# Sum of the expert outputs, normalisation and second projection in one block, the list in the experts' block, and semaphores cleared a stage later

## The reference

```
scores = softmax(x @ router_w + expert_bias); top_w, top_idx = top_k(scores, 4); top_w /= sum(top_w)
out_k  = (silu(x @ gate[k]) * (x @ up[k])) @ down[k]            # 16 experts
ffn    = sum over the 4 chosen k of top_w[k] * out_k
x      = x + layernorm(ffn)                                      # layer 2
h      = layernorm(x); q, k, v = h @ Wq.T, h @ Wk.T, h @ Wv.T    # 32 heads of 8
f      = log_sigmoid(h @ Wf.T + bf); c = cumsum(f)               # float32
scores = q k / sqrt(8) + c_i - c_j, causal, softmax, times v, @ Wo.T
```

## Time and profile before

| | |
|---|---|
| runs | 1692.95, 1695.21, 1696.98 us; median 1695.21 |
| profiled execution | 1693.19 us, of which the span is 1691.2 us |
| mean granted TensorE clock | 0.788 of full |
| busy over the span | PE 1168.4, DVE 1196.8, ACT 886.3, POOL 422.6 us |
| router | 513.2 to 564 us |
| expert loop | 567 to 768 us |
| combine, n2, clear, qkv1 | 774.4 to 923.2 us |
| attention a1 | 923.2 to 1450 us |

### The profile page before, as it was taken

How to read it: one execution, slowest core, us unless ns; L and a number is a source line. 1 busy time by engine, 2 the same in 40 slices (tenths; PEclk the granted TensorE clock), 3 DMA queues, 4 the chain that set the end, 5 groups by cost and what they waited for, 6 DMA issues and landing times. The chain is left out here.

```text
span 1691.2 us, 26266 instructions
## 1 busy us (share of the span) xinstructions
PE 1168.4 (69%) x7624; PEld 567.9 (34%) x7701; DVE 1196.8 (71%) x3589; ACT 886.3 (52%) x1731; POOL 422.6 (25%) x565
## 2 busy tenths in 40 slices
PE   2456555556532599991183899999999999737995
PEld 1112221122221366660151233333333333323664
DVE  4799999999848444445647888888888887355443
ACT  2698898888761243332341366566666666233212
POOL 0212212221114577771120122222222222010000
PEclk9655555555555799995587799999999999768997
DMA  2255665666514122226065111111111110201001
GB/s 66 82 120 115 125 132 110 117 129 119 98 44 93 41 78 79 78 80 217 0 241 196 54 38 58 57 39 57 57 40 56 58 41 29 78 0 23 1 1 50
DMA packets 221546, 130.96 MB, mean 77 GB/s; under 512 B 167990, under 2 KB 194742, under 8 KB 221150
## 3 DMA queue, kind: packets, MB, share of 16 engines
q1 hardware_dynamic: 200942, 100.17, 23.8%
q0 software_dynamic: 6320, 15.54, 2.9%
q10 hardware_dynamic: 14144, 13.57, 2.8%
HBM read 54.51 MB, written 40.76 MB: 56 GB/s over the span
## 5 line engine op out<-in xcount | busy, mean ns | idle before, releaser
L884 ACT ACTIVATE a_probs<-a_st 128x1024 f32<-128x1024 f32 (+3 forms) x256 | 212.4, 865 | 158.5 <-PE a_st L816 158.5
L938 DVE CUSTOM_DVE_ANT_0 a_unread<-a_row,all_mask 128x128 bf16<-128x128 f32 (+3 forms) x512 | 238.7, 485 | 32.8 <-PE a_row L781 28.0
L781 PE MATMUL a_row<-l_k,a_q 128*128 128x512 bf16 (+3 forms) x736 | 229.9, 334 | 45.4 <-DMA l_k<-k_rows 27.3
L816 PE MATMUL a_st<-a_q,l_k 128*128 128x384 bf16 (+3 forms) x735 | 224.0, 327 | 26.4 <-ACT a_probs L884 24.3
L653 DVE CUSTOM_DVE_ANT_0 a_rows<-a_sc,all_mask 128x128 bf16<-128x128 f32 (+7 forms) x256 | 191.5, 748 | 22.1 <-PE a_sc L507 21.1
L912 POOL TENSOR_SCALAR_AFFINE_SELECT a_probs<-a_probs 128x256 f32<-128x256 f32 x256 | 102.5, 406 | 412.3 <-ACT a_probs L884 336.3
L556 ACT ACTIVATE a_rows<-a_rows 128x128 bf16<-128x128 bf16 (+7 forms) x256 | 173.2, 677 | 61.1 <-DVE a_rows L663 57.1
L942 DVE TENSOR_REDUCE a_mx<-a_row 128x1 f32<-128x512 f32 x256 | 175.9, 687 | 38.4 <-PE a_row L781 38.4
L507 PE MATMUL a_sc<-a_k,a_q 16*128 16x512 bf16 (+3 forms) x384 | 167.2, 504 | 49.8 <-DVE a_mx L653 43.1
L835 PE MATMUL a_o<-a_probs,a_v 128*32 128x384 f32 (+3 forms) x1920 | 176.6, 431 | 0.0
L565 ACT ACTIVATE a_unread<-a_rows 128x128 bf16<-128x128 bf16 (+7 forms) x256 | 170.7, 667 | 0.0
(11 more groups left out here) (247 smaller groups left out, 1849.2 us busy)
## 6 DMA issues: line engine op xcount, KB each, us to landing
a_q<-q_rows SPq DMA_DIRECT2D x64, 128.0 KB
l_k<-k_rows SPq DMA_DIRECT2D x64, 128.0 KB
o_rows<-a_oT SPq DMA_DIRECT2D x32, 256.0 KB, 2.0
a_turned_sb<-a_rows SPq DMA_TRANSPOSE x256, 2.6
sum_made<-out_rows SPq DMA_DIRECT2D x8, 512.0 KB, 9.3
sum_made<-out_rows ACTq DMA_DIRECT2D x8, 512.0 KB, 8.5
a_raw<-in_gate ACTq DMA_DIRECT2D x16, 224.0 KB, 3.4
a_raw<-in_up ACTq DMA_DIRECT2D x16, 224.0 KB, 4.1
```

Source lines behind the costliest of these rows:

```text
L781: nc.tensor.matmul(row[:, n % SLOTS, 0:w], q_sb[:, u % RING, POS[qb] * P:(POS[qb] + 1) * P], k_sb[:, u % RING, h, lo:lo + w], start=True, ...
L816: last = nc.tensor.matmul(st[:, n % 2, to + first:to + end], k_sb[:, u % RING, h, kb * P:(kb + 1) * P], q_sb[:, u % RING, first:end], star ...
L884: nc.scalar.activation(probs[:, n % GR, lo:hi], st[:, n % 2, lo:hi], ACT.Exp).then_inc(exp_done, 1)
L938: nc.vector.tensor_tensor_reduce(out=unread[:, n % SLOTS, 0:w], in0=tile[:, 0:w], in1=mask[:, at:at + w], scale=1.0, scalar=-3e38, op0=ALU ...
```

## The change

1. Instead of `clear`, `retire()` only sets the semaphores of the stages so far aside. `wipe(pool)`, a call within POOL's queue of a later stage, clears them: after the first memset of the experts' block, after the memsets of the new sum block, after the first copy of attention a1, and at the end of POOL's queue in the int8 network. The clear at the very end stays.
2. `router` and `experts` are one Block. PE waits on `which_ready` before the loop. The four operations that make `chosen` are the function `weigh()`, called in DVE's loop ahead of tile 4. Part of SBUF and PSUM is shared between list and loop.
3. The eight constant stores of the tails are in the experts' block, on SP between the tables and the down weights, with a wait for their landing ahead of the down weights.
4. `combine`, n2 and `qkv1` become `sum_and_project`. Tiles are taken in the order in which the attention wants its blocks (`tile_at`), in four groups of four; statistics, root and normalisation are per group (`Spread`), the second normalisation is on ACT. The orders of the queues are written out by hand. Items of q and k go by batch half. The gate is on 64 partitions x 1024. ACT now rounds straight from PSUM to the first part, DVE subtracts it from PSUM: two DVE operations and two ACT operations per item, where there were four and one. Stores go per 512 columns; q is stored in three planes only. All loads are issued by SP, the weights after four tiles.
5. `load` of attention a1 reads planes 0 and 1 of q more than once: eight transfers per unit instead of four.

```diff
-        clear(nc)                       # three places
+        retire()
...
+def wipe(pool):
+    for s in Core.stale:
+        pool.sem_clear(s)
...
@@ experts
+            tails(sp)
             sp.dma_start(wd[:], ...).then_inc(wd_loaded, 16)
...
+            pe.wait_ge(which_ready, 1)
+            for i in range(TILES + 3):
...
             nc.gpsimd.memset(every[:], 1.0).then_inc(ones_set, 1)
+            wipe(pool)
...
+            nc.vector.tensor_scalar(which[:], endsum[:], float(E - 1), None, ALU.min).then_inc(which_ready, 1)
             for i in range(TILES + 1):
+                if i == 4:
+                    weigh()
...
@@ sum_and_project, SP
+            for p in range(GT): load(p)
+            (weights)
+            for p in range(GT, T): load(p)
+            for i in range(len(todo)):
+                store(i)
+                if i == len(todo) - 5:
+                    sp.wait_ge(f_chain, 7)
+                    sp.dma_start(c_v[:, 0:3], cparts[:]).then_inc(c_stored, 16)
@@ PE, per half s
+                turn(2 * s); gate(2 * s)
+                if s + 1 == B: turn(2 * s + 1); gate(2 * s + 1)
+                project(first); project(first + 1); value(2 * s)
+                if s + 1 < B:
+                    turn(1); gate(1); project(2); project(3); value(1); project(4 .. 7)
+                else:
+                    project(10 .. 15); value(3)
@@ PE, project(i)
+                if i >= 2: pe.wait_ge(remains, i - 1)
@@ ACT
+            def norm_y(g):
+                act.wait_ge(of_y.nmi_ready, g + 1)
+            def round_high(i):
+                act.wait_ge(acc_ready, i + 1)
+                nc.scalar.mul(parts[:, i % pring, 0], acc[:, i % 2], scale[todo[i][0]]).then_inc(high, 1)
+            def round_middle(i):
+                act.wait_ge(remains, i + 1)
+                nc.scalar.copy(parts[:, i % pring, 1], rest[:, i % pring]).then_inc(middle, 1)
+            def split_pair(i): round_high(i); round_high(i + 1); round_middle(i); round_middle(i + 1)
+            scale_first(0), scale_first(1), norm_y(0), scale_first(2), norm_y(1), norm_x(0), copy_x(0),
+            scale_first(3), split_pair(0), copy_v(0), norm_x(1), norm_y(2), copy_x(1), split_pair(2),
+            copy_v(1), norm_x(2), norm_y(3), split_pair(4), split_pair(6), copy_x(2), norm_x(3), copy_x(3),
+            split_pair(8), copy_v(2), gate_step(0 .. 3), split_pair(10), (12), (14), copy_v(3)
@@ POOL
+            wipe(pool)
+            of_y.root(0), of_y.root(1), of_x.root(0), of_y.root(2), of_x.root(1), of_y.root(3), of_x.root(2), of_x.root(3)
@@ DVE
+            def less_high(i):
+                dve.wait_ge(high, i + 1)
+                nc.vector.scalar_tensor_tensor(out=rest[:, i % pring], in0=acc[:, i % 2], scalar=scale[todo[i][0]],
+                                               in1=parts[:, i % pring, 0], op0=ALU.mult, op1=ALU.subtract).then_inc(remains, 1)
+            def less_middle(i):
+                dve.wait_ge(middle, i + 1)
+                nc.vector.tensor_tensor(out=parts[:, i % pring, 2], in0=rest[:, i % pring], in1=parts[:, i % pring, 1],
+                                        op=ALU.subtract).then_inc(low, 1)
+            def split_pair(i): less_high(i); less_high(i + 1); less_middle(i); less_middle(i + 1)
+            combine(0), invert y0, combine(1), residual(0), invert y1, x0, combine(2), residual(1), invert y2, x1,
+            split_pair(0), combine(3), residual(2), invert y3, x2, split_pair(2), residual(3), invert x3,
+            split_pair(4), (6), (8), gate_step(0 .. 6), split_pair(10), (12), (14)
...
@@ attention a1, load
-                for sb, rows in ((q, q_rows), (k[:, h], k_rows)):
-                    sp.dma_start(sb[64 * h:64 * (h + 1), :], rows (8 planes x 8 rows))
+                for first, count, plane in ((0, 3, 0), (3, 2, 1)):
+                    sp.dma_start(q[64 * h + first * hd:64 * h + (first + count) * hd, :],
+                                 q_v[plane:plane + 1].broadcast_to([count, hd, S])).then_inc(sem, 16)
+                sp.dma_start(q[64 * h + 5 * hd:64 * (h + 1), :], q_v[5:8]).then_inc(sem, 16)
+                sp.dma_start(k[64 * h:64 * (h + 1), h, :], k_v).then_inc(sem, 16)
```

More of the change, by code:

```diff
@@ L1305, in gather_of, with experts @@
     return gather
-def router(nc, a, lg, wd, wd_loaded, chosen, which, source, target, gather):
+def experts(nc, a, lg, wparts, wd, wd_loaded, chosen, which, source, target, taken, gathered, gather, ident_f, ident_b, out_rows, tails):
     with ExitStack() as ctx:
-        c = Core(nc, ctx, "route")
+        c = Core(nc, ctx, "moe")
         later = c.sb("later", [P, P], BF16)
@@ new lines, with tile_at, natural_pieces, projections @@
+STORES = {"q": 2, "k": 3}
+def tile_at(p):
+    return p // TB * TB + ORDER[p % TB]
+def natural_pieces(j):
+    out = []
+    for m, blk in enumerate(range(4 * j, 4 * j + 4)):
+        if out and POS[blk] == out[-1][2] + out[-1][1]:
+            out[-1][1] += 1
+        else:
+            out.append([m, 1, POS[blk]])
+    return out
+def projections():
+    out = []
+    for s in range(B):
+        out += [("q", s, j, ch) for j in range(2) for ch in range(KC)]
+        out += [("k", s, j, ch) for j in range(2) for ch in range(KC)]
+    return out
@@ L1658, in _ @@
         @block.scalar
         def _(act):
-            for t in range(1, ring, 2):
-                load(act, t)
-            for t in range(T):
-                act.wait_ge(loaded[t % ring], 16 * (t // ring + 1))
-                if t >= 2:
-                    act.wait_ge(added, 3 * (t - 1) - 2)
-                nc.scalar.activation(part[:, t % 2, 0], made[:, t % ring, 0, :], ACT.Identity,
-                                     scale=chosen[:, t, 0:1]).then_inc(scaled, 1)
-                if t % 2 == 0 and t and t + ring - 1 < T:
-                    load(act, t + ring - 1)
@@ L1823, in _, with split_pair @@
-            nc.scalar.activation(unread[:], za[:, 0:1], ACT.Exp, scale=-1.0)
+            def split_pair(i):
+                round_high(i)
+                round_high(i + 1)
+                round_middle(i)
+                round_middle(i + 1)
+            scale_first(0)
+            scale_first(1)
+            norm_y(0)
+            scale_first(2)
+            norm_y(1)
+            norm_x(0)
+            copy_x(0)
+            scale_first(3)
+            split_pair(0)
+            copy_v(0)
@@ new lines, in _ @@
+            norm_x(1)
+            norm_y(2)
+            copy_x(1)
+            split_pair(2)
+            copy_v(1)
+            norm_x(2)
+            norm_y(3)
+            split_pair(4)
+            split_pair(6)
+            copy_x(2)
+            norm_x(3)
+            copy_x(3)
+            split_pair(8)
+            copy_v(2)
+            for i in range(4):
+                gate_step(i)
+            split_pair(10)
+            split_pair(12)
+            split_pair(14)
+            copy_v(3)
@@ new lines, in _ @@
+            combine(2)
+            residual(1)
+            of_y.invert(dve, 2)
+            of_x.invert(dve, 1)
+            split_pair(0)
+            combine(3)
+            residual(2)
+            of_y.invert(dve, 3)
+            of_x.invert(dve, 2)
+            split_pair(2)
+            residual(3)
+            of_x.invert(dve, 3)
+            split_pair(4)
+            split_pair(6)
+            split_pair(8)
+            for i in range(7):
+                gate_step(i)
+            split_pair(10)
```

700 lines of the change are left out of this document (397 added, 303 removed).

## The result

The changed kernel takes 1656.6 us (median of 4, 1655.3 to 1660.2) against 1695.2: the ratio is 0.978, 95% interval [0.976, 0.980], faster by 38.6 us where 1656 and 38.0 were forecast. The profiled execution is the slowest of the four (1660.2, span 1658.5); against the span before of 1691.2 it gains only 32.7. The first attention, whose code is the same, ended later in it, and this has to be set apart before stages are compared.

The account below looks back on a forecast made before the run. No single bound: no engine busy above 71%. Clears 6.0, loop 8.0, stretch 21.6, last clear 5.0, less a1 loads 2.6, gain 38.0 on 1693.19 us: 1655.2, median put at 1656, range 1643 to 1674.

Parts of the forecast that it names:

- (a): Stretch from sum to attention: DVE waits 5.5 us until the first tile has landed.
- (b): Same stretch: DVE waits for five roots at about 1.1 us each, 5.5 us.
- (c): Same stretch: DVE's residual(3) waits 4.5 us for norm_y(3), which stands behind other work on ACT.
- (e): Same stretch: DVE waits 10 us at item 8 for ACT's copies and normalisation, PE's last turns, gate and projection.
- (f): Same stretch: DVE waits 1.1 us at item 9.
- (g): Same stretch: DVE's gate steps wait 7.4 us for ACT's copy_v(2), four gate steps and a table load.
- (d): Same stretch: DVE waits 1.2 us at item 7 for PE, 1.9 us per item against 1.4 on DVE.
- (h): Same stretch: DVE waits 2.1 us at items 12 to 15, at PE's pace.
- the clock term: Same stretch: PE's clock can fall while it waits, slowing the next items; 6.7 us at most, 3 taken.
- the slow clock: Rival: PE stays at the lower clock through the stretch, 35 us more, 1691 us; chance 5%.
- The orders did lock more than I saw: Rival: hand-written orders lock ACT and DVE more, (c) and (e) each 8 us longer, loop gaining only 5: 1675; 13%.
- the slow rival: Rival: SP can't keep up with a1's eight loads per unit; at 2.3 us per load 50 us more, 1706; 3%.

Follow-up runs that it names:

- two Blocks: Changed kernel with list and expert loop in two Blocks again and the weights made at the end of the list: 1664.1 us, ratio 0.981 to the kernel before.
- the second trace of the kernel before: The kernel before, run again unedited on a fast chip: ratio 0.9995, first gather to last scatter 213.39 us.
- the third order: Changed kernel with the projection's queues reordered, a1 loads in four transfers, weight operations spread over tiles 8 to 32: 1639.6 us, ratio 0.968 to the kernel before.
- the repeated changed kernel: Changed kernel run again unedited on a slow chip: 1694 us, ratio 0.976 to the kernel before.
- the last two kernels: The third order, 1639.6 us, and the same with a1's constant step rows loaded in the block before, 1635.4 us, ratio 0.964 to the kernel before.

## Why the prediction was right, step by step

- *Clears*: right. 6.15 and 4.85 of 6.0 and 5.0; a plain end costs 0.46 to 0.53, not the 0.32 of the earlier trace rows and far from the 3.3 of the list's end, and a semaphore 0.077 to 0.082, not 0.085.
- *Loop*: right in each part. Scatter 0 was 10.3 earlier, `weigh` cost 2.09, the sum was 8.8 for 8.0; two Blocks gave 8.8 back. By the second trace of the kernel before (213.39) the gain is 7.5, so 8 is right within what one trace can tell. What I left out is the 0.7 at the loop's end, 7.88 for 7.21, which the two Blocks gave back too.
- *Stretch*: 127.6 for 127.5, but from errors that cancel, so that an agreement to 0.1 is luck. (a) 4.5 for 5.5, (b) 4.8 for 5.5, (c) 4.50 for 4.5, (e) 8.50 for 10, (f) 1.03 for 1.1, (g) 7.59 for 7.4 held. (d) was 4.35 for 1.2, (h) 5.07 for 2.1, and 2.72 at items 2 and 3 weren't foreseen: PE was slower there, with the granted clock at 0.54 in 815 to 820, 0.50 in 835 to 840 and again in 865 to 875. That is the clock term, taken as 3 and worth 6.4 (next point). Without it the waits are 36.6 for the 37 of full clock, with it 43.0 where I had 40. DVE's own work was 120.5 - 43.0 = 77.5 for 81: a residual with its statistics goes every 0.67 us, 10.7 for the sixteen and not 13.1, and a pair of items takes 2.6, 20.7 for eight and not 22.6. Two of my sums were wrong besides: the terms of (c) add up to 4.9 and not 4.5 (4.50 was measured), and the fast end, full clock with the old tail, is 123.8 and not 122.5.
- *What the clock cost* is in the rows. PE makes the pair of items 6 and 7, and again 12 and 13, with the same instructions in every order. From PE's start to ACT's second rounding the two pairs took 6.35 and 6.25 us in the changed kernel, with the first item of each at a granted clock of 0.50 (the lower of the two levels, 1.2 GHz for 2.4), and 3.67 and 3.71 in the third order at 1.00. Item 2 took 3.2 at 0.61 for 2.0 at 1.00. That is 2.7 + 2.5 + 1.2 = 6.4, all at places where DVE waits for PE. PE's rows of items 6 and 7, first in the changed kernel, then in the third order:

```profile
834.78 6.31 PE L1836 MATMUL qkv_acc<-qkv_xT,qkv_w 128*128 128x128 f32 x16 [4.94 <-DVE qkv_rest L2026]
824.18 3.64 PE L1846 MATMUL qkv_acc<-qkv_xT,qkv_w 128*128 128x128 f32 x16
```

- *Tail*: 7.2 for 6.5.
- *Median*: 1656.6 for 1656. Counted strictly, 1655.2 and the 2.0 by which the profiled execution lay under the median give 1657.2; either is within the 0.2% of a measurement.
- *Loads of a1*: 2.65 for 2.6; undoing them gave 2.8 to 3.1. In 895 to 905 the DMA share was 0.24 and 0.28 with 79 and 89 GB/s, before 0.53. The Trainium skill, "DMA: Bandwidth & Descriptors", Rules for kernel authors, says that a leading broadcast of c copies confines a transfer to at most c engines, and the low shares agree with it. No trace tells the two prices of a piece, by engines or by size, apart.
- *Rivals*: the clock did fall but rose again each time, so the slow clock cost 6.4 and not 38. The orders did lock more than I saw in one respect: not against my forecast, but against what the block could do, by 18 us. SP's eight loads take 5.6 us of a unit's 15.8, so the slow rival was far off.

## What to carry to other kernels

Where several in-order queues are written out by hand, write down for each wait what the releaser itself waits for. The waits in the projection were all put down to ACT and had three sources: PE behind a turn and a gate that the next product didn't need (8.50), ACT behind its own copies of v and gate steps (4.50 and 7.59), and PE at the lower clock after it had stood (items 6, 7, 12 and 13). Moving one product ahead took 6.8 us off one wait and put 5.9 on the next; an order that as a whole feeds PE in a fixed pattern, with the gate later, took 18 us off. A block that exists only to clear semaphores costs its count times 0.08 us on every engine; the same clears in the queue of an engine that has nothing to do showed no cost.

## What the runs showed of the hardware

The kernel before took 1695 us on two chips and 1736 and 1741 on two others. Traces of the slow chips exist only of the changed kernel and its variants, and there nearly all of the difference is the expert loop: from scatter to scatter 2.43 to 2.47 us per tile on the fast chips, 2.93 to 3.05 on the slow chips, with POOL's operations as long as before (0.97 and 0.99). In the repeated changed kernel POOL waits 1.8 us instead of 0.30 at every third scatter, 0.49 us per tile, which is the whole of it. PE's and ACT's rows there:

```profile
642.56 0.37 ACT L1507 COPY moe_shared<-moe_dn 128x256 f32<-128x256 f32 x1 [0.89 <-PE moe_dn L1466]
643.95 1.03 PE L1466 MATMUL moe_dn<-ride_wd,moe_shared 112*128 x4
648.35 0.37 ACT L1507 COPY moe_shared<-moe_dn 128x256 f32<-128x256 f32 x1 [3.94 <-PE moe_dn L1466]
```

And ACT's longest such wait on a fast chip, in the first trace of the changed kernel:

```profile
657.71 0.37 ACT L1507 COPY moe_shared<-moe_dn 128x256 f32<-128x256 f32 x1 [3.55 <-DMA out_rows<-moe_shared,ride_target]
```

The copy waits for two things, PE's product and the landing of the scatter of four tiles earlier (`OUT` is 4). On the fast chips it is the landing that ends the long waits, up to 3.6 us, and POOL isn't delayed. On the slow chip it seems to be the landing too, since PE's product ends at 644.98 by its row. The semaphore records of the trace say otherwise: the increment of PE's product is recorded at 648.33, 3.35 us behind that end, with those of the next five of PE's steps within 0.27 us behind it, and ACT starts 0.02 us after it. The scatter in question, issued at 635.78, has its last recorded increment at 638.60. About half of PE's increments in the loop come more than 0.5 us behind the end in their row on the slow chips (126 to 158 of 304 in each of the eight traces); on the fast chips none does (of 305 in each of six traces). Only about a quarter of the landings' increments are in the traces of the slow chips, but the last recorded one of a scatter lies at a median of 2.3 us behind its issue, on the fast chips 2.4. So nothing in the traces points to slower landings, and a longer ring wouldn't have ended this wait sooner: PE's signals come late. As ends of matrix products are modelled in a profile, the records don't tell whether PE itself stood or only its increments were late, and why stays open.

Second, the granted clock differs between executions of the same code. Item 2, with the same orders ahead of it in the changed kernel and five variants, took 2.0 us at a clock of 1.00 in one trace and 3.2 at 0.61 in another; between the last two kernels, the same up to the new loads, such shifts moved a stretch of 110 us by 2.7.
